# Selection products of the CoPE attention, split over four row groups of TensorE

## The reference

```python
def cope(query, attn_logits, pos_emb):            # pos_emb: 32 x 64
    gates = jax.nn.sigmoid(attn_logits)
    pos = jnp.flip(jnp.cumsum(jnp.flip(gates, axis=-1), axis=-1), axis=-1)
    pos = jnp.minimum(pos, npos_max - 1)
    pos_ceil, pos_floor = jnp.ceil(pos).astype(jnp.int32), jnp.floor(pos).astype(jnp.int32)
    logits_int = jnp.einsum('bhqd,dn->bhqn', query, pos_emb)
    logits_ceil = jnp.take_along_axis(logits_int, pos_ceil, axis=-1)
    logits_floor = jnp.take_along_axis(logits_int, pos_floor, axis=-1)
    w = pos - pos_floor
    return logits_ceil * w + logits_floor * (1.0 - w)
# per head: 16 heads, batch 4, 1024 queries, 1024 keys, head dimension 32
logits = jnp.einsum('bhqd,bhkd->bhqk', Q, K) / jnp.sqrt(d)
scores = jax.nn.softmax(logits + cope(Q, logits, pos_emb), axis=-1)
out = jnp.einsum('bhqk,bhkd->bhqd', scores, V)
```

## Time and profile before

| | us |
|---|---|
| median of 3 runs | 15340.84 (15337.57 to 15372.86) |
| the profiled execution | 15370.8 |
| its span in the trace | 15369.1 |

### The profile page before, as it was taken

How to read it: one execution, slowest core, us unless ns; L and a number is a source line. 1 busy time by engine, 2 the same in 40 slices (tenths; PEclk the granted TensorE clock), 3 DMA queues, 4 the chain that set the end, 5 groups by cost and what they waited for, 6 DMA issues and landing times. The chain is left out here.

```text
span 15369.1 us, 176674 instructions
## 1 busy us (share of the span) xinstructions
PE 12799.3 (83%) x57462; PEld 8566.0 (56%) x57462; DVE 7438.2 (48%) x13140; ACT 4440.7 (29%) x7890; POOL 6509.8 (42%) x5384
## 2 busy tenths in 40 slices
PE   8878999999667888888888888888888888888845
PEld 3554333333445666666666666666666666666622
DVE  0112222232225666666666666666666666666633
ACT  0111222222113333333333333333333333333310
POOL 0000000000005666666666666666666666666600
PEclk9888988888777888888888888888888888888866
DMA  3111000000113333333333333333333333333223
GB/s 81 44 46 29 21 19 20 20 20 20 59 57 70 81 81 81 81 81 81 81 81 81 80 80 80 81 81 79 81 81 80 82 80 80 81 81 81 69 69 100
DMA packets 1037896, 1029.79 MB, mean 67 GB/s; under 512 B 738306, under 2 KB 845570, under 8 KB 972306
## 3 DMA queue, kind: packets, MB, share of 16 engines
q1 hardware_dynamic: 964114, 1020.70, 27.7%
q10 hardware_dynamic: 73728, 8.42, 0.4%
HBM read 817.83 MB, written 210.76 MB: 67 GB/s over the span
## 5 line engine op out<-in xcount | busy, mean ns | idle before, releaser
L916 PE MATMUL c_pickps<-c_table,c_hot 128*128 128x112 f32 x16384 | 3464.9, 388 | 563.3 <-DVE c_over L1207 541.9
L916 PEld LDWEIGHTS c_pickps<-c_table,c_hot 128*128 128x128 f32 x16384 | 3296.3, 265 | 667.6 <-DVE c_over L1207 569.3
L1297 POOL TENSOR_TENSOR c_total<-c_total,c_over 128x384 f32<-128x384 f32 (+3 forms) x3584 | 3284.0, 916 | 476.8 <-DVE c_over L1207 197.5
L1184 DVE COPY_PREDICATED c_pickps<-c_upper,c_pickps 128x256 f32<-128x256 uint32 (+1 forms) x1024 | 799.0, 826 | 3349.3 <-PE c_pickps L916 3349.3
L1297 POOL TENSOR_TENSOR c_total<-c_total,c_middle 128x1024 f32<-128x1024 f32 x512 | 1210.0, 2363 | 2853.6 <-DVE c_middle L1198 2853.6
L1264 POOL IOTA c_digitrow<- 1x128 f32 x1 | 0.3, 255 | 4614.4 <-POOLq L65 4614.4
L1049 ACT ACTIVATE c_over<-c_place,c_thresholds 128x384 f32<-128x384 f32 (+3 forms) x3584 | 1589.2, 525 | 0.0
L1207 DVE TENSOR_TENSOR c_over<-c_over,c_pickps 128x384 f32<-128x384 f32 (+3 forms) x3584 | 1407.1, 452 | 0.0
L1032 ACT ACTIVATE c_place<-c_gateps 128x512 f32<-128x512 f32 x1024 | 611.4, 597 | 2674.2 <-PE c_gateps L889 2674.1
L510 DVE TENSOR_REDUCE a_max<-a_peakps 128x1 f32<-128x1024 f32 x512 | 627.0, 1225 | 1202.7 <-PE a_peakps L442 1202.7
L464 PE MATMUL a_outps<-a_probs,a_v 128*128 128x512 f32 x2048 | 1201.5, 716 | 0.3 <-DVE a_outT L522 0.3
(11 more groups left out here) (213 smaller groups left out, 14832.8 us busy)
## 6 DMA issues: line engine op xcount, KB each, us to landing
c_hot<-t_digits SPq DMA_DIRECT2D x512, 1024.0 KB
t_tables<-c_tablesb SPq DMA_DIRECT2D x256, 256.0 KB, 5.1
c_table<-t_tables SPq DMA_DIRECT2D x1024, 56.0 KB, 2.3
c_kb<-t_kb SPq DMA_DIRECT2D x256, 128.0 KB, 6.1
t_digits<-c_anchorrows SPq DMA_DIRECT2D x128, 256.0 KB, 2.4
a_q<-t_qa SPq DMA_DIRECT2D x128, 128.0 KB, 2.4
a_k<-t_ka SPq DMA_DIRECT2D x128, 128.0 KB, 2.5
c_ka<-t_kb SPq DMA_DIRECT2D x128, 128.0 KB, 5.6
```

Source lines behind the costliest of these rows:

```text
L916: mm = nc.tensor.matmul(pick_ps[:, h // 4, 0:WIDTH, r * 8:(r + 1) * 8], hot[t % 2][:, h, :], table[s][:, :, :, t * 16 + h].rearrange("p l ...
L1184: ins = nc.vector.copy_predicated(pick_ps[:, :, at:at + width, :], far.unsqueeze(2).to_broadcast([128, 4, width, 32]), pick_ps[:, :, at + ...
L1297: nc.gpsimd.tensor_tensor(a, a, b, ALU.add).then_inc(s_add, 1)
```

## The change

Each product of a pick is cut into four over 32 rows. Row group g holds lanes 2g and 2g + 1, so of the 112 columns only the 28 of these two lanes are streamed through it, and each group writes to a PSUM bank of its own. For that, the queries of a tile are numbered by lane: query = 16 x lane + h, where it was 8 x h + lane. The table copy (ACT), the anchor subtraction (DVE) and the output columns of the pick follow this numbering. Waits, semaphores, buffers and transfers are the same.

```diff
                     if h == 8 and turn is not None:
                         turn_anchor(turn)
-                    r = h % 4
-                    mm = nc.tensor.matmul(pick_ps[:, h // 4, 0:WIDTH, r * 8:(r + 1) * 8], hot[t % 2][:, h, :],
-                                          table[s][:, :, :, t * 16 + h].rearrange("p l m -> p m l"), start=True, stop=True)
+                    for g in range(4):
+                        rows, lanes = slice(32 * g, 32 * g + 32), slice(2 * g, 2 * g + 2)
+                        mm = nc.tensor.matmul(pick_ps[:, g, 0:WIDTH, h:32:16], hot[t % 2][rows, h, :],
+                                              table[s][rows, lanes, :, t * 16 + h].rearrange("p l m -> p m l"),
+                                              start=True, stop=True)
                 mm.then_inc(s_pickps, 1)
@@ keep_table
-                nc.scalar.activation(table_sb[n][:, :].rearrange("p (l x) -> p l x", l=8), gate_ps[:, :].rearrange("p (x l) -> p l x", l=8),
-                                     ACT.Copy).then_inc(s_tablesb, 1)
+                nc.scalar.activation(table_sb[n][:, :].rearrange("p (l t h) -> p l t h", l=8, t=4),
+                                     gate_ps[:, :].rearrange("p (t l h) -> p l t h", t=4, l=8), ACT.Copy).then_inc(s_tablesb, 1)
@@ near
-                nc.vector.tensor_scalar(anchor[:, :].rearrange("p (t l h) -> p t h l", t=4, l=8),
-                                        rounded[:, :].rearrange("p (t h l) -> p t h l", t=4, l=8), EIGHTS, None, ALU.subtract).then_inc(s_anchor, 1)
+                nc.vector.tensor_scalar(anchor[:, :], rounded[:, :], EIGHTS, None, ALU.subtract).then_inc(s_anchor, 1)
```

## The result

The changed kernel takes 16221.43 us (median of 4 runs, 16194.81 to 16267.22) against 15356.85 for the kernel before in the same comparison: ratio 1.0561, 95% interval 1.0524 to 1.0599. It is slower, in the direction of the forecast (15790, which is 449 above the kernel before), by 865 us, about twice as much, and within the stated range. The profiled execution has a span of 16238.2 us and a mean granted clock of 0.746, where before it was 0.846.

What follows compares the result with a forecast made beforehand. Bound: PE's picks and DVE's work taking turns, 77.2 us a quad. 15370.8 us profiled, +370 for the clock and +75 for instructions, gave 15816, or 15790 as a median; own range 15450 to 16250, wider range 14500 to 16700.

Steps and rivals of the forecast that it cites:

- PE and DVE take turns: Kernel's bound: a pick on PE, DVE's work in the one pick_ps, the next pick; 77.2 us a quad, 19.3 a tile.
- Price of a pick: Split picks on PE: four groups load and stream side by side, 3.8 us at full clock, 7.2 us at half.
- rival 3: Picks on PE: weight loads stand in line, 14.3 us a pick at full clock, 18,700 us or more; chance 0.04.
- rival 2: Picks on PE: issue at 56 ns a pair becomes the bound, 7.4 us a pick, 16315 us; chance 0.20.
- The clock: PE: narrow picks don't raise the clock and let it fall, add_cope starts at half; +2.9 us a quad, +370 us.
- Rival 1: Picks on PE: four groups hold the clock, all picks take 3.8 us at full level, 14235 us; chance 0.24.
- The 0.75 that I gave for tile 2's pick: Granted clock during tile 2's pick before the change, which took 6.70 us; 6.5 was expected after.
- On tile 3 my terms: Tile 3's period: anchor turns at half clock +0.4 us, shorter anchor subtraction -0.5; rounded to +0.1.
- The anchor subtraction: DVE, on tile 3's chain: unstrided after the change, it goes from 1.20 to 0.69 us, -0.5 us.
- Instructions: PE's loop body grows from 1344 to 2880 loads and matmuls and may be fetched again each pass; 1.2 us, +75 in all.
- the queue in front of the array hides most of it: PE at each loop pass: queued work mostly hides the instruction fetch, leaving 1.2 us a pass.
- The ceiling, 3.46 us a pass for one transfer: Upper bound for instruction fetch on PE's path, taken from DVE's wait for the hot load; +220 us in all.

Runs made afterwards that it cites:

- narrow-stream run: Kernel before with whole-array 128-row products that each stream 28 columns instead of 112, without the row split: 15668.72 us, ratio 1.0197.
- wide-stream run: Changed kernel, but each of the four row groups streams all 112 columns instead of its own 28: 15853.36 us, ratio 1.0331 to the kernel before.
- body of four quads: Kernel before with a loop body of four quads instead of two in all engines, same work and order: 15430.5 us, ratio 1.0049.

## Why the prediction was right, and what was off

The mechanism held: the narrow pick neither brings the clock back nor keeps it, and add_cope pays. The size came out at about half of the measured one. That the time still lies in the forecast's own range of 15450 to 16250 is partly luck, since the code's share left its bounds.

- *PE and DVE take turns* was right: DVE waits for picks in 469 places, and what a pick or an add_cope gains or loses shows in the period.
- *Price of a pick* was right: rounds of 112 ns at full and 215 at half, four groups side by side. The means are 7.04, 4.33 and 6.47 us for tiles 0 to 2; I had taken 7.2, 4.4 and 6.5. Loads in a line (rival 3) and an issue limit of 56 ns a pair (rival 2) are out: a pair comes every 28 ns. (The logits' pace is (1.16 - 0.27) / 15 = 59 ns and not 56; a time for 16 records holds 15 intervals.)
- *The clock* was right in place and sign. The narrow-stream run, which has nothing else, gives +2.4 us a quad where I had +2.9. Rival 1, that four busy groups hold the clock, is out. add_cope at half cost 1.9 us each, where L894's record said 1.8. I had charged it to six of ten on tile 1, and 84% are at half. I had also charged add_cope alone, but the gate product behind it (L889) still takes about 1.4 us there instead of 1.0. These two make most of the way from -0.8 to -0.2. The 0.75 that I gave for tile 2's pick is not in the rows that I named; the trace has it (0.75 from 9076.1 to 9082.8 us). On tile 3 my terms gave +0.4 - 0.5 = -0.1, which I rounded to +0.1; it was +0.9.
- *The anchor subtraction* was wrong: I had read one row of 1.20 against its neighbour's 0.69 and charged -0.5 us. Unstrided, its median is 993 ns (first fence), strided 944 (the kernel before, second fence; duration min/median/max in ns); the means are 901 and 1023, so it gained about 0.1 us. The same unstrided instruction has a median of 740 ns in the wide-stream run, so something else than the stride sets most of its time. The shortest of each kernel, 428 and 601 ns, is the first of the stage and the only one that runs while POOL does nothing; that POOL's work makes the others longer was not tested.

```profile
L1166 DVE TENSOR_SCALAR c_anchor<-c_rounded x128: 428/993/1196, 4723.7 to 15356.6; 128x512 f32<-128x512 f32 x128
```

```profile
L1164 DVE TENSOR_SCALAR c_anchor<-c_rounded x128: 601/944/1227, 4677.0 to 14496.7; 128x512 f32<-128x512 f32 x128
```

- *Instructions* was the most mis-sized term, and the main reason why the forecast is half of the result. I had +75 us, within bounds of 0 to 220. The wide-stream run, which has the change's code and not its narrow stream, is 413 us longer in the stage; about 100 of them are add_cope at half behind the pause, which the change's clock term has already. The change's own trace shows 3.3 us on tile 0 and 1.0 on tile 3 more in the first quad of a pass than in the second, together about 4.2 us a pass and 260 us in all. What failed is the step that the queue in front of the array hides most of it: PE stands 2.7 us at each branch. (In the body of four quads, two passes of three have no pause; in the change none is without.) The ceiling, 3.46 us a pass for one transfer, holds for this pause in the mean, but not for what hangs on it: the rest of the 3.3 us, and tile 3's wait for the hot load. (The loop has 62 passes, not 63.) Another 200 us are the 1.6 us a quad on tiles 1 and 2 that only the change has, and for which I had no term. Here the Trainium skill (Runtime: NRT & Kernel Launch, Instruction fetch mechanics) had named the mechanism, and the packets bear it out: 28 to 30 at bodies of 1403 and 1535, 424 and 900 at 2803 and 2939. At 1915, under the 2048 that the page gives, there were 583, so the measurement puts the limit for a loop body lower, between 1535 and 1915.

The other rule that I weighed, that of TensorEngine Tiling (Array Packing), Performance Considerations, of the Trainium skill, speaks against splitting a dimension that is already small. In this kernel passes of 28 columns cost nothing by their size, since they lie under the loads. The split was a loss for another reason than the page's: with 28 columns the mean granted clock fell from 0.846 to 0.746.

## What to carry to other kernels

A matmul that is bound by its weight load isn't made cheaper by splitting its rows, and its wide stream may be what keeps the clock up for the work behind it: look at the granted clock behind a stage before shortening the stage. Split where the clock is already held by dense work ahead, and only there. Count the instructions of a loop body before multiplying products, and look at the packets of the instruction queue after.

## What the runs showed of the hardware that I had not expected

- At full clock a record of two passes of 112 columns takes 192 ns, and the same load with 56 or 28 columns 112 ns; at half all take 215. That 112 columns take so long may be due to their stride, which no run varied.
- Loads and matmuls of four row groups of 32 run side by side; starts within a round are 6 to 8 ns apart.
- A body of 1535 instructions on PE stays, one of 1915 is fetched again in every pass (30 against 583 packets), and the first tile of a pass was then longer by 1.7 us with 2803 instructions, 1.9 with 1915 and 3.3 to 4.9 with 2939. The pause ahead of add_cope in it was 0.9, 1.7 and 2.6 to 2.7 us in the mean. Where there was a pause, PE went on 1.6 to 1.9 us (means of four kernels) after the last packet had landed, and add_cope was mostly at half clock.
- The same unstrided fp32 subtraction of 128 x 512 on DVE took between 426 and 1006 ns in one run (median 740) and had a median of 993 in another; strided, 601 to 1227 (median 944). One row says little about what such an instruction costs.
